# A new order of the five engines in the first and last channel mixes of a macaron block

## The reference

```
x = x + 0.5 * ffn(layernorm(x))          # FFN1
x = x + retention(layernorm(x))          # RET
x = x + 0.5 * ffn(layernorm(x))          # FFN2, the same weights

ffn(x):   x_prev = x shifted by one token
          xr = mu_r*x + (1-mu_r)*x_prev;  xk = mu_k*x + (1-mu_k)*x_prev
          r  = sigmoid(xr @ W_r.T);       k  = relu(xk @ W_k.T)**2
          out = r * (k @ W_v.T)
retention(x): 8 heads of 32; q, k, v = x@Wq, x@Wk, x@Wv; chunks of 64 tokens
          attn = (q k^T) * decay;  o = attn v + (q*decay_q) S;  S = decay_s*S + (k*decay_k)^T v
          out = o @ Wo
```

## Time and profile before

| | us |
|---|---|
| median of three executions | 339.76 (339.11 to 339.87) |
| the profiled execution, its own time | 338.8 |
| its span, first to last instruction | 336.9 |
| TensorE busy in the span | 322.3 |
| VectorE busy | 297.0 |
| ScalarE busy | 210.5 |
| GpSimd busy | 135.1 |

### The profile page before, as it was taken

One profiled execution on the slowest core, in us unless ns is written; L12 is line 12 of the kernel. 1 busy time (PEld: TensorE's weight loads), 2 busy tenths in 40 slices (PEclk: granted clock), 3 DMA queues, 4 the chain that ended last, 5 costly groups with the idle time before them and its releaser, 6 DMA issues.

```text
span 336.9 us, 11291 instructions
## 1 busy us (share of the span) xinstructions
PE 322.3 (96%) x4260; PEld 302.4 (90%) x4260; DVE 297.0 (88%) x696; ACT 210.5 (62%) x422; POOL 135.1 (40%) x242
## 2 busy tenths in 40 slices
PE   4979999999999999999999999999999999999975
PEld 4869899999999999999899999989999998989874
DVE  4989899999999999899999989999897979888954
ACT  2877556775757586674758567475857555374362
POOL 4386165608163451706245270715424154221130
PEclk9999999999999999999999999999999999999999
DMA  7610010102001020201102020100000010000001
GB/s 232 247 35 31 4 34 0 34 5 62 4 2 63 2 65 3 65 2 27 41 3 64 2 63 2 53 16 32 2 19 17 2 35 7 26 4 31 34 2 62
DMA packets 11556, 12.08 MB, mean 36 GB/s; under 512 B 1008, under 2 KB 11120, under 8 KB 11504
## 3 DMA queue, kind: packets, MB, share of 16 engines
q1 hardware_dynamic: 11072, 11.18, 10.4%
q10 hardware_dynamic: 432, 0.20, 0.2%
...
## 4 chain that ended last, share of the span: by engine, by line
PE 88%; DVE 4%; issue 3%; ACT 2%; POOL 1%; DMA 1%; ACTq 0%; DVEq 0%; POOLq 0%
PE psum L964 39%; PE psum L956 24%; PE psum L948 7%; PE psum L1035 5%; PE psum L1067 5%; PE psum L1054 3%; PE psum L1025 2%; PE psum L1080 2%; PE psum L1157 1%; DMA ident<-in_ident 1%; ACT xn L344 1%; DVE stats L624 1%; PE psum L1161 1%; PE psum L1127 1%; PE psum L1115 0%
## 5 line engine op out<-in xcount | busy, mean ns | idle before, releaser
L199 POOL TENSOR_TENSOR xr_lo<-xrT,xr_hi 128x512 fp32r<-128x512 f32 x24 | 41.1, 1728 | 99.8 <-ACT xr_hi L375 99.8
L344 ACT ACTIVATE xn<-x,shift,rstd 128x256 f32<-128x256 f32 x96 | 52.0, 591 | 10.1 <-POOL shift L283 10.1
L692 DVE TENSOR_TENSOR attn<-psum,decay 128x512 f32<-128x512 f32 x64 | 42.4, 683 | 4.7 <-PE psum L1035 4.7
L964 PE MATMUL psum<-w_hi,xr_hi 128*128 128x256 f32 x124 | 38.6, 312 | 1.7 <-DVE xr_lo L199 1.2
L624 DVE BATCH_NORM_STATS2 stats<-x 128x6 f32<-128x256 f32 x96 | 35.7, 414 | 4.9 <-DMA x<-in_x 4.6
L276 POOL TENSOR_TENSOR var_eps<-moments,eps 128x2 f32<-128x2 f32 x48 | 18.9, 395 | 43.7 <-DVE moments L628 42.9
L964 PE MATMUL psum<-w_hi,ka_hi 128*128 128x256 f32 x120 | 35.7, 297 | 0.7 <-ACT rgate L403 0.7
L956 PE MATMUL psum<-xa_hi,w_hi 128*128 128x256 f32 x128 | 35.8, 280 | 0.0
L956 PE MATMUL psum<-xk_hi,w_hi 128*128 128x256 f32 x120 | 34.5, 288 | 1.1 <-POOL xk_lo L193 0.9
L956 PE MATMUL psum<-xa_lo,w_hi 128*128 128x256 f32 x128 | 35.5, 278 | 0.0
L956 PE MATMUL psum<-xa_hi,w_lo 128*128 128x256 f32 x128 | 35.5, 277 | 0.0
...
## 6 DMA issues: line engine op xcount, KB each, us to landing
...
```

The source lines that it names most:

```text
L199: engine.tensor_tensor(xr_lo[f][n % 2][:], xrT[f][n % 2][:], xr_hi[f][n % 2][:].bitcast(F32), ALU.subtract).then_inc(xr_lo_ready[f], 1)
L344: act.activation(xn[s][n % 2][:, t, :], x[n % len(x)][:, t, :], ACT.Identity, bias=shift[s][n % 2][:, t:t + 1], scale=rstd[s][n % 2][:, t: ...
L692: dve.tensor_tensor(attn[r][:], bank[B_SCORES[r]].rearrange("p (g c i) -> p g c i", g=G, c=TILES), decay[:, r, :, :].unsqueeze(2).broadcas ...
L964: mm = pe.matmul(halves(b)[:, t, :], xt[:, g, cols], wt[:, g, :], start=(j == 0), stop=(j == 5))
```

## The change

Eight things change.

1. For two blocks, FFN1's first and FFN2's last (the set `FAST`), VectorE makes the normalised rows: `layer_stats` ends with `var_eps` on VectorE, GpSimd does only the power (`rstd`), and a new function `normalize_fast` writes `xn` with two `tensor_scalar` instructions, (x - mean) * rstd. `minus_mean`, `shift` and ScalarE's two instructions go away for these two blocks.
2. `warm_up` multiplies a tile of zeros, set by GpSimd's first memset, and so no longer waits for the load of `ident`. There are 12 such matmuls ahead of the first transpose and 7 behind it; there were 14, 13 and 3 transposes.
3. The weight splits move: W_K's high part from VectorE to ScalarE, W_Q's high part from ScalarE to GpSimd, W_KEY's low part from GpSimd to VectorE, and those of W_K, W_V and W_R to other places of VectorE's list.
4. In the fill FFN1's block 2 comes later everywhere: `transpose_T(FFN1, 2)` and `hidden(FFN1, 2)` used to stand ahead of `gate(FFN1, 1)`; now the transpose stands just ahead of that gate, and the matmuls behind the first `outer`.
5. Some low parts go to another engine: to GpSimd `xr_low` of FFN1 blocks 1 and 2 and of FFN2 blocks 11 and 12, `xk_low` of FFN1 blocks 3 and 15, `square_low` of FFN1 block 3 and FFN2 blocks 11, 13 and 15 (both halves); to VectorE `square_low` of FFN1 blocks 2 and 15 and FFN2 block 12, `xk_low` of FFN1 block 4, `add_ffn` of FFN1 blocks 14 and 15, and (from ScalarE) `square` of FFN2 block 0.
6. In the drain `relu(FFN1, 15)` moves up in ScalarE's list, ahead of `normalize(FFN2, 12)`.
7. In the drain `xr_low(FFN2, 14)` moves up in VectorE's list, ahead of `o_low(15)`, `add_retention(15)` and the last statistics.
8. `keep_warm` runs 16 matmuls instead of 18, and the last blocks' halves use other PSUM banks.

The loop body is the same. The core of the diff; a line or two stand for each table of calls:

```diff
+        zeros = sb("zeros", [P])
...
-        B_HID_1, B_OUT_1 = {FFN1: 0, FFN2: 4}, {FFN1: 4, FFN2: 0}
+        B_HID_1, B_OUT_1 = {FFN1: 4, FFN2: 5}, {FFN1: 1, FFN2: 2}
...
+        FAST = {(FFN1, 0), (FFN2, 15)}
+
+        def shifts(s, n):
+            return sum((s, k) not in FAST for k in range(n))
...
             def inverse_std(s, n):
                 m = moments[s][n % 2]
+                if (s, n) not in FAST:
+                    pool.wait_ge(moments_ready[s], 2 * n + 2)
+                    if (s, n - 2) in FAST:
+                        pool.wait_ge(rstd_ready[s], n - 1)
+                    pool.tensor_tensor(var_eps[s][n % 2][:], m[:, :, 1], eps[:], ALU.add).then_inc(var_ready[s], 1)
+                    pool.tensor_tensor(minus_mean[s][n % 2][:], m[:, :, 0], minus_one[:], ALU.mult).then_inc(minus_mean_ready[s], 1)
                 pool.wait_ge(xn_ready[s], max(2 * (n - 1), 0))
                 pool.wait_ge(var_ready[s], n + 1)
                 pool.tensor_tensor(rstd[s][n % 2][:], var_eps[s][n % 2][:], exponent[:], ALU.pow).then_inc(rstd_ready[s], 1)
+                if (s, n) not in FAST:
+                    pool.wait_ge(rstd_ready[s], n + 1)
+                    pool.wait_ge(minus_mean_ready[s], shifts(s, n + 1))
+                    pool.tensor_tensor(shift[s][n % 2][:], minus_mean[s][n % 2][:], rstd[s][n % 2][:], ALU.mult).then_inc(shift_ready[s], 1)
+            pool.memset(zeros[:], 0.0).then_inc(zeros_set, 1)
...
+            square_low(pool, FFN2, 15, part=0)
+            square_low(pool, FFN2, 15, part=1)
...
-            normalize(FFN1, 0, x0)
+            split_high_act(W_K)
...
+                if (s, n) in FAST:
+                    dve.wait_ge(constants_set, 3)
+                    dve.wait_ge(moments_ready[s], 2 * n + 2)
+                    dve.wait_ge(rstd_ready[s], max(n - 1, 0))
+                    dve.tensor_tensor(var_eps[s][n % 2][:], moments[s][n % 2][:, :, 1], eps[:], ALU.add).then_inc(var_ready[s], 1)
+
+            def normalize_fast(s, n, x):
+                dve.wait_ge(rstd_ready[s], n + 1)
+                dve.wait_ge(xnT_psum[s], max(n - 1, 0))
+                for t in range(TILES):
+                    dve.tensor_scalar(xn[s][n % 2][:, t, :], x[n % len(x)][:, t, :], moments[s][n % 2][:, t, 0:1],
+                                      rstd[s][n % 2][:, t:t + 1], ALU.subtract, ALU.mult).then_inc(xn_ready[s], 1)
...
             def warm_up(b, count):
-                pe.wait_ge(ident_loaded, 16)
+                pe.wait_ge(zeros_set, 1)
                 for _ in range(count):
-                    pe.transpose(bank[b][:, 0:P], ident[:], ident[:])
+                    pe.matmul(bank[b][:, 0:P], zeros[:], zeros[:], start=True, stop=True)
...
-            keep_warm(3, 18)
             pe.wait_ge(xnT_ready[FFN2], 15)
+            keep_warm(B_T[FFN2], 16)
             transpose_T(FFN2, 15)
```

More of the change, by code:

```diff
@@ L310, in _ @@
             inverse_std(FFN1, 5)
[L311 removed]
+            square_low(pool, FFN1, 3)
+            xr_low(pool, FFN2, 0)
+            inverse_std(FFN2, 1)
             xr_low(pool, FFN1, 4)
[L313 to L314 removed]
             inverse_std(RET, 3)
@@ L848, in _ @@
             update_state(1, 12)
+            decayed_query(13)
+            gate(FFN1, 14)
             add_ffn(dve, FFN2, 10)
+            add_retention(12)
             mix_r(FFN1, 15)
-            xk_low(dve, FFN1, 15)
-            decayed_query(13)
-            add_retention(12)
+            add_ffn(dve, FFN1, 14)
             layer_stats(FFN2, 12, x2)
-            xr_low(dve, FFN2, 11)
+            layer_stats(RET, 14, x1)
+            square(dve, FFN1, 15)
+            mask_scores(3, 13)
@@ L871, in _ @@
-            update_state(1, 13)
-            xa_low(14)
-            xr_low(dve, FFN2, 12)
+            mask_scores(0, 13)
+            mask_scores(1, 13)
+            mask_scores(2, 13)
+            square_low(dve, FFN1, 15)
+            update_state(0, 13)
+            scale_state(1, 13)
+            update_state(1, 13)
+            difference(FFN2, 12)
+            xa_low(14)
+            mix_r(FFN2, 12)
+            mix_k(FFN2, 12)
+            scale_state(0, 14)
+            xk_low(dve, FFN2, 12)
@@ L1284, in _ @@
             hidden(FFN2, 0, 1)
+            key(2, 1)
+            pe.wait_ge(relu_ready[FFN1], 4)
+            hidden(FFN1, 4, 0)
             hidden(FFN1, 4, 1)
```

449 lines of the change are left out of this document (213 added, 236 removed).

## The result

The kernel after takes 336.06 us (335.76 to 336.37, four executions), the kernel before in the same comparison 339.44 (338.98 to 339.87): ratio 0.9901, interval 0.9882 to 0.9919. The change makes it 3.4 us or 1% faster; the forecast was 2.0, and the measured time lies 0.14 under its range. The profiled execution took 336.37 with a span of 334.3 (before 338.8 and 336.9), so between the two profiled executions there are 2.4 us (2.6 in the span, as 2.1 lie outside it for 1.9), and 1.0 more between the medians, which no trace of the pair can show.

The account below looks back on a forecast made before the run. TensorE is always busy from 26.5 to 268 us, so only head, fill and drain count: 0.6 (fill) + 0.5 (relu) + 1.0 (last block's chain) - 0.1 (last product) = 2.0, from 339.76 to 337.75. Range 336.2 to 339.6.

Parts of the forecast that it names:

- The offset: Last step: before's profiled execution is 0.96 below the median of the runs, so 0.96 also separates after's 336.8 from 337.75.
- The head: Before TensorE's first transpose: power 0.7, pair of `tensor_scalar` 0.6, transpose at 6.3 instead of 7.90, covered by dummies.
- The fill's mechanism: Up to the loop: VectorE's list sets the times, the head's 1.6 lead shrinks; 0.6 gained, bounds 1.6 and -1.0.
- three gaps of 1 to 1.5: Sign in the fill: TensorE has three gaps near 1 to 1.5 us between 15.5 and 22.
- waits before `xa_lo` and `ka_lo`: End of the fill, block 2: about 0.25 before `xa_lo` and 0.15 before `ka_lo`, against 0.05 now.
- the rival that the fill gives nothing: Low parts on VectorE's list and GpSimd eat the head's lead before `key` and `query`; 338.35, chance 0.18.
- The relu: Drain: TensorE's stall of 0.57 for `relu(FFN1, 15)` goes; 0.5 gained, bounds 0.57 and -0.3.
- The last block's chain: Drain, `scores(15)` to last transpose: `xr_low` costs 0.6, fast normalisation gains; 1.0 gained in sum, bounds 1.3 and 0.5.
- The last product: End of the drain: GpSimd makes `square_low(15)` in two halves, 0.75 each; 0.1 lost, 0.8 late if 1.19 each.
- the rival that the drain gives nothing: Power and halves on GpSimd cost 1.10 and 1.19, `o_low` late by 0.6 and more; 339.1, chance 0.10.
- Slower by the clock: Rival: TensorE's clock falls in the fill's gaps for some three blocks of 12 matmuls, 4.3 more; 342.0, chance 0.10.
- a fill of 1.2 with the drain at its better bounds: Case behind the lower end of the range, 336.2: fill gains 1.2, drain's terms at their better bounds.

Follow-up runs that it names:

- v_xrlow: Kernel after with VectorE's `xr_low(FFN2, 14)` moved from ahead of `o_low(15)` to between the last statistics and `normalize_fast`, 4 dummies instead of 16: 336.63 us, ratio 0.9907.
- head_norm: Kernel before with only the fast normalisation of FFN1's block 0 on VectorE and the dummies of zeros: 340.54 us, ratio 1.0032.
- a_no_dummies: Kernel after with one dummy of zeros in place of 12 and none in place of 7: 338.56 us, ratio 0.9969.

## Why the prediction was wrong, point by point

- **The step that failed**: "It is 0.96 below the median of the runs, so that goes from 339.76 to 337.75". In its own scale the sum was 336.8 and the profiled execution took 336.37, 0.4 off. The offset was carried over as if it belonged to the kernel. It belonged to the draw: after's profiled execution lies 0.31 above its median, not 0.96 below. That is 1.27 of the 1.69 missed. The kernel before spreads over 3.5 us, from its fill and its loop, the kernel after over 0.6 in ten executions. By the times shown before one could see only 1.1 of it (338.80 to 339.87), but the range had no term for it. It was in part chance that the error was so large: another profiled execution of before would have had another offset.
- **The head, right.** First transpose 6.36 (forecast 6.3), power 0.70 (0.7), pair 0.73 (0.6), dummies done 0.75 before it. The Trainium skill's double rate for float32 `tensor_scalar` (VectorE: DVE Perf Modes, "The perf-mode tier table", given there for 2048 elements) does not show at this size: the pair of 256 columns took 0.73, a pair of two-input sums 0.75.
- **The fill's mechanism, right in the main; the size of its term, too small.** `hidden(FFN1, 1)` 16.37 (15.9), `gate(FFN1, 1)` 19.58 (19.1), RET's first transpose 21.87 (22.05). About 0.4 of the lateness of the first two is the landing of block 1's rows, 7.10 where 6.72 was taken. TensorE waits 1.12 and 0.64 before the last two and nothing before the first, where three gaps of 1 to 1.5 were told. The forecast took 0.3 off the lead of 0.9 for waits before `xa_lo` and `ka_lo`; of these only 0.14 was there. The pair of traces has 0.88, the mean of the traces 1.2, the medians 1.4 to 1.9, for **0.6**. Its upper bound of 1.6 was the better number, and the rival that the fill gives nothing fell.
- **The relu, right** in the two traces and alone in the kernel before (0.65 and 0.6 for 0.5), but its bounds were not those of the move inside this change: without it the drain's new lists lose 1.4.
- **The last block's chain: the number right, one cause wrong.** 1.2 for 1.0; from the moments to the transpose 1.96 (2.0 to 2.4 was the sign), with the dummies ending last (the last transpose at 321.49, `xn` done at 321.38). `o_lo` came 0.6 later against `scores(15)` as told (6.84 behind its start for 6.25), but v_xrlow shows that this is not VectorE's `xr_low`: `o_lo` waits for ScalarE's `o_hi` with it or without, and that for TensorE's product.
- **The last product, right**: GpSimd's two halves took 1.41 together and TensorE waited for `rgate` as before; about -0.1 in all. With that and the power at 0.69 the rival that the drain gives nothing fell too.
- **Slower by the clock, did not happen** in after. A stretch at the lower clock is in head_norm, where it accounts for some 0.3 of the 1.0 lost, and by the durations in a_no_dummies, which is 2.4 slower.
- **The range.** Its lower end, 336.2, was put down to a fill of 1.2 with the drain at its better bounds. That is 1.2 + 0.57 + 1.3 = 3.1, or 336.7.

Open: how much of the old fill's spread is VectorE and GpSimd meeting. The rows show it in two of nine executions and made on purpose. The wait that takes away one meeting leaves the median within 0.5, and in its trace another GpSimd instruction, the power near 10 us, made the fill late. The means of the traces give 1.2 + 1.7 = 2.9 of the 3.4 measured; the last 0.5 may be chance in which executions were profiled.
